# Third convolution: own-shift fetches of two chunks ahead of one burst of sixteen row transfers

## The chip, the cores and the metric

The kernel runs on one core of a Trainium2 chip. The metric is device time in microseconds (us) of one launch, the median of several runs. The core has TensorE (PE in the profile), VectorE (DVE), ScalarE (ACT), GpSimd (POOL) and SyncE (SP). SP and GpSimd issue the DMAs here: SP plain ones, GpSimd the indirect ones, whose rows are picked by an index in each partition.

## The reference, cut to what matters

A graph network with 6,250 nodes of 32 features and 200,000 edges sorted by destination: a spline-convolution layer (two small convolutions make a shift `t` per node, a third convolution uses it) and then a message-passing layer.

```
h = relu(layernorm(x))
h1 = elu(spline_conv(ones, row, col, basis, idx, stn1_w, stn1_b))
h2 = elu(spline_conv(h1, row, col, basis, idx, stn2_w, stn2_b))
t  = elu(h2 @ stn3_w + stn3_b) @ stn4_w + stn4_b
new_pseudo = clip(pseudo + t[col] - t[row], 0, 1)
basis2, idx2 = spline_basis(new_pseudo)
x = x + spline_conv(h, row, col, basis2, idx2, conv_w, conv_b)
...
mi = zeros.at[dst].add(e * x[src]);  mo = zeros.at[src].add(e * x[dst])
x = x + tanh-MLP(concat(mi, mo, h))
```

`t[row]` is an edge's own shift: all edges of one group of 16 slots have the same source node, so one fetched row per group gives it.

## The kernel before

The stages run one after the other, with barriers between them: `sort_edges`, `first_conv`, `second_conv`, `shift_network`, `third_conv`, `end_first_layer`, `bucket_rows` and `second_layer`. The change touches `third_conv` alone (lines 1765 to 2181).

`third_conv` works through 148 chunks (`NCK`) of 2,048 edge slots. Each engine has its own program, and semaphores are all that order them:

- **PE** (lines 2088 to 2181) does four rounds per chunk. In a round stand 32 matmuls of `outer_products` for chunk k+1 (line 2125), 16 of `weigh` for chunk k (line 2138) and 24 of `gather` for chunk k+3 (line 2105). Once per chunk it folds (2147), sums over nodes (2154) and spreads the own shifts of chunk k+3 (2113).
- **DVE** (1890 to 2035) is in chunk k with work for later chunks: `choose`, `own_shifts`, `take_own` and `move` for chunk k+3, `make_outer` and `make_basis` for chunk k+2, in two parts each. `own_shifts` (1957) reads the fetched own shifts, `take_own` (1962) copies what PE spread, and `make_basis` ends with `near_apart` (1982), which sets `s_basis`.
- **ACT** (2038 to 2085) copies PE's products out of PSUM (2042) and makes the hats.
- **SP** (1832 to 1860) waits in step k for the whole basis of chunk k-2 (`s_basis`, line 1848). Then it loads the near rows of chunk k (1849), waits until slot k mod 4 of the sending buffers is free, and loads eight rows per partition of edge data with their places (1852, 1853; `s_in`).
- **GpSimd** (1863 to 1887) does two unrelated things in one program, in a loop of four chunks (`DEEP`). It fetches the own shifts of chunk k from `t_rows` in HBM (1877) into one of two buffers, and it sends eight rows per partition of the edges into their buckets in HBM (`edges_b`, 1883), one indirect DMA for each row (`STEP` is 8). The sends serve the second layer and are not read in this stage. The fetch waits for `s_wide`, which tells that DVE has read the own shifts of chunk k-2, so that the buffer is free. The sends wait for `s_in`.

The order on GpSimd before, for each chunk: wait for the buffer, fetch; wait for the loads, eight sends. `second_conv` does some of the same sends (1453, sixteen in each pair of chunks of its last part) and, before them, gathers of 32 per pair of chunks (1431).

Of the kernel before, what the change touches and what calls it, by code (L numbers as in the profile page):

```python
# [58 lines left out]
STEP = 8  # L59
DEEP = 4  # L60
# [61 lines left out]
def held(pool, name, most):  # L122

    reg = pool.alloc_register(name)
    pool.reg_mov(reg, most)
    return pool.snap(reg)
# [1638 lines left out]
def third_conv(g, c, x, w_dram):  # L1765
# [19 lines left out]
    sending = Sending(g, c, "c3")  # L1785
# [4 lines left out]
    own_idx = sb("own_idx", [P, DEEP], U32)  # L1790
    own, own_wide, own_pos = sb("own_shift", [P, 2, 4]), sb("own_wide", [P, CH, 3]), sb("own_pos", [P, CH, 3])
# [7 lines left out]
    s_back, s_row, s_own = ([sm(f"{n}{h}") for h in range(2)] for n in ("near_in", "dst_rows", "own_shifts_sent"))  # L1799
    s_own_idx = sm("own_idx")  # L1800
    s_tick, s_pe_turn = sm("turns"), sm("pe_turns")
# [3 lines left out]
    s_wide, s_spread, s_taken = sm("own_wide"), sm("own_spread"), sm("own_taken")  # L1805
# [24 lines left out]
    with nc.Block() as block:  # L1830
        @block.sync
        def _(sp):
            sp.wait_ge(s_set, 1)
            sp.dma_start(weights[:, :, :], w_dram).then_inc(s_w, 16)
            sp.dma_start(g.x[:, 0:FULL_BLK, :], x[0:FULL_BLK * P, :].rearrange("(b p) f -> p b f", p=P)).then_inc(s_x, 16)
            sp.dma_start(g.x[0:REST, FULL_BLK, :], x[FULL_BLK * P:N, :]).then_inc(s_x, 16)

            def dst_rows(k, half):
                sp.dma_start(rows[:, half, :], g.dst_rows[ds(k * CH, CH), :].rearrange("t e -> (t e)").unsqueeze(0)
                             .to_broadcast([P, CH * P])).then_inc(s_row[half], 16)  # L1840

            def four_chunks(i, last):
                for n in range(DEEP):
                    k = i * DEEP + n
                    if not last or n < DEEP - 2:
                        sp.wait_ge(s_dst, k + 1)
                        dst_rows(k + 2, n % 2)
                    sp.wait_ge(s_basis, k * 2 + 2)
                    sp.dma_start(near[:, n % 2, :, :], near_rows[:, ds(k * CH, CH), :]).then_inc(s_back[n % 2], 16)
                    sp.wait_ge(sending.s_sent[n], i * (STEP * 16) + 16)  # L1850
                    step = i * DEEP + (EARLY + n)
                    sp.dma_start(sending.rows[:, n, :, :], edge_rows[:, ds(step * STEP, STEP), :]).then_inc(sending.s_in[n], 16)
                    sp.dma_start(sending.idx[:, n, :], edge_idx[:, ds(step * STEP, STEP)]).then_inc(sending.s_in[n], 16)

            for half in range(2):
                dst_rows(half, half)
            with sp.Fori(0, NCK // DEEP - 1) as i:
                four_chunks(i, False)
            four_chunks(NCK // DEEP - 1, True)
            sp.wait_ge(s_x, 32)  # L1860

        @block.gpsimd
        def _(pool):
            g.open_sent(pool, sending.s_sent)
            g.open_sent(pool, s_own, DEEP)
            last_node, last_place = held(pool, "last_node_of_t", NBLK * P - 1), held(pool, "last_place", P * NT - 1)
            with pool.Fori(0, NCK // DEEP) as i:
                for half in range(2):
                    pool.wait_ge(s_own[half], i * 32 + 16)
                pool.tensor_copy(own_idx[:, :], g.group_n[:, ds(i * DEEP, DEEP)]).then_inc(s_own_idx, 1)  # L1870
                pool.wait_ge(s_own_idx, i + 1)
                for n in range(DEEP):
                    k = i * DEEP + n
                    pool.wait_ge(s_own[n % 2], i * 32 + (n // 2 * 16 + 16))
                    pool.wait_ge(s_wide, k + 1)
                    pool.sem_inc(s_tick, 1)
                    pool.indirect_dma_start(own[:, n % 2, :], None, g.t_rows,
                                            bass.IndirectOffsetOnAxis(own_idx[:, n:n + 1], 0),
                                            bounds_check=last_node, oob_is_err=False).then_inc(s_own[n % 2], 16)
                    pool.wait_ge(sending.s_in[n], i * 32 + 32)  # L1880
                    pool.sem_inc(s_tick, 1)
                    for q in range(STEP):
                        pool.indirect_dma_start(g.edges_b, bass.IndirectOffsetOnAxis(sending.idx[:, n, q:q + 1], 0),  # L1883
                                                sending.rows[:, n, q, :], None, bounds_check=last_place,
                                                oob_is_err=False).then_inc(sending.s_sent[n], 16)
            for n in range(DEEP):
                pool.wait_ge(sending.s_sent[n], NCK // DEEP * (STEP * 16) + 16)

# [775 lines left out]
```

## Time and profile before

| | us |
|---|---|
| median of 3 runs | 11131.68 |
| lowest and highest run | 11116.91, 11136.16 |
| profiled execution, first to last instruction (span) | 14339.7 |
| PE busy in that span | 10087.9 (70%) |
| DVE, ACT busy | 7530.8 (53%), 4613.2 (32%) |
| GpSimd busy | 6070.4 (42%) |
| third convolution in the span | about 8530 to 11982 |

The profile gives no time of the profiled execution other than its span. The span is 3208 us longer than the median of the runs, so a duration of the profile isn't at once a duration of the runs. Start times are counted from the span's first instruction. "Issue" is idle time of an engine in which it waited for nothing that the profile shows.

### The profile page before, as it was taken

The numbers are of one execution on the slowest core, as the hardware profiler recorded it, in microseconds if no ns is written. First come the engines' busy times: TensorE is split into PE (matmuls) and PEld (weight loads), VectorE is DVE, ScalarE is ACT, GpSimd is POOL, SyncE is SP. The second block draws the span as 40 slices with busy tenths as digits, with TensorE's granted clock in tenths as the row PEclk, the third lists the DMA queues.
The fourth block names the chain that finished last, engine by engine and source line by source line (L and its number), as shares of the span: only waits on it lengthen the run. The fifth ranks groups of instructions, "written<-read, shape, count | busy, mean of one in ns | idle before, by whom it ended". The sixth has DMA issues, their size and how long they took to land. (4 is left out here: it accounts for less than half of the span.)

```text
span 14339.7 us, 414245 instructions
## 1 busy us (share of the span) xinstructions
PE 10087.9 (70%) x156361; PEld 8506.1 (59%) x156362; DVE 7530.8 (53%) x18528; ACT 4613.2 (32%) x11707; POOL 6070.4 (42%) x5974
## 2 busy tenths in 40 slices
PE   7566666657366666666677757777787776888888
PEld 7556555546244444444565545666666665888887
DVE  6667666757333333333344434444444444777776
ACT  0001000035122222222233322222222224777776
POOL 0477777743455545455433314444444441111111
PEclk6555555555566666666777767777777776555555
DMA  0222223310222222222211111111111112444443
GB/s 32 45 62 67 64 62 64 64 31 8 76 74 74 74 74 75 74 74 74 69 42 48 42 27 37 35 36 36 35 36 36 34 36 57 115 116 116 115 115 91
DMA packets 850556, 875.92 MB, mean 61 GB/s; under 512 B 629005, under 2 KB 632517, under 8 KB 849966
## 3 DMA queue, kind: packets, MB, share of 16 engines
q1 hardware_dynamic: 622830, 526.55, 13.2%
q0 software_dynamic: 227648, 348.32, 9.9%
q8 instruction: 50, 0.82, 0.0%
q14 instruction: 28, 0.23, 0.0%
HBM read 631.25 MB, written 135.27 MB: 53 GB/s over the span
## 5 line engine op out<-in xcount | busy, mean ns | idle before, releaser
L1611 PE MATMUL c_py<-c_products,c_weights 125*64 125x128 f32 x18944 | 1630.8, 302 | 675.0 <-issue 669.7
L769 POOL DMA_INDIRECT edges_by_rank<-rank_stage,rank_idx x1568 | 1844.7, 1176 | 602.0 <-issue 575.0
L1883 POOL DMA_INDIRECT edges_b<-c_send_rows,c_send_idx x1184 | 1277.9, 1079 | 1902.8 <-DMA c_send_idx<-edge_idx 1586.7
L1556 ACT ACTIVATE c_products<-c_pa 125x512 f32<-125x512 f32 x2368 | 1222.8, 602 | 2391.5 <-remote 1424.9
L1600 PE MATMUL c_pa<-c_near_apart,c_basis 32*125 32x128 f32 x18944 | 1247.0, 315 | 983.2 <-issue 734.5
L1611 PEld LDWEIGHTS c_py<-c_products,c_weights 125*64 125x64 f32 x18944 | 1236.6, 150 | 982.9 <-issue 927.2
L1431 POOL DMA_INDIRECT c_near_ranked<-h_rows,c_idx x1568 | 1597.9, 1019 | 478.1 <-issue 477.8
L1516 DVE TENSOR_TENSOR c_basis<-c_outer,c_hats 128x1000 f32<-128x1000 f32 x296 | 355.4, 1201 | 2745.9 <-PE c_pa L1600 2229.3
L1600 PEld LDWEIGHTS c_pa<-c_near_apart,c_basis 32*125 32x125 f32 x18944 | 958.5, 208 | 1297.4 <-issue 1295.7
L2042 ACT ACTIVATE c_products<-c_pa 125x256 f32<-125x256 f32 x2368 | 713.9, 386 | 2275.5 <-PE c_pa L2125 1411.0
L2125 PE MATMUL c_pa<-c_near_apart,c_basis 32*125 32x128 f32 x18944 | 1180.9, 334 | 242.7 <-issue 201.3
L289 PE MATMUL acc_s<-hot_col,hot_row 128*123 128x91 f16 x3136 | 768.4, 409 | 707.5 <-DVE same_a L668 416.0
L2488 PE MATMUL acc_mi_mo<-msg,hot_e 128*128 128x32 bf16 x8768 | 1152.6, 205 | 154.0 <-issue 153.0
L289 PEld LDWEIGHTS acc_s<-hot_col,hot_row 128*123 128x123 f16 x3136 | 723.4, 319 | 760.6 <-DVE same_a L668 442.3
L2125 PEld LDWEIGHTS c_pa<-c_near_apart,c_basis 32*125 32x125 f32 x18944 | 920.9, 223 | 422.1 <-issue 384.2
L748 PE MATMUL pg_s<-start_table,hot_turned 123*128 123x91 f32 x3136 | 1059.1, 450 | 136.3 <-issue 135.8
L2349 POOL DMA_DIRECT2D rows<-local_rows x548 | 298.9, 546 | 2000.3 <-DVE hot_d L2367 1819.7
L2488 PE MATMUL acc_mi_mo<-msg_low,hot_e 128*128 128x32 bf16 x8768 | 1143.2, 188 | 0.6 <-issue 0.6
L2488 PE MATMUL acc_mi_mo<-msg_rest,hot_e 128*128 128x32 bf16 x8768 | 1143.3, 188 | 0.0
L2105 PE MATMUL c_pt<-t_parts,c_dst_hot 128*128 128x78 bf16 x14208 | 850.3, 218 | 403.7 <-issue 351.1
L2105 PEld LDWEIGHTS c_pt<-t_parts,c_dst_hot 128*128 128x128 bf16 x14208 | 681.7, 110 | 637.6 <-issue 635.5
L2488 PEld LDWEIGHTS acc_mi_mo<-msg,hot_e 128*128 128x128 bf16 x8768 | 911.1, 104 | 212.2 <-issue 209.9
(402 smaller groups left out, 21318.8 us busy)
## 6 DMA issues: line engine op xcount, KB each, us to landing
rows<-local_rows POOLq DMA_DIRECT2D x548, 256.0 KB, 4.1
own_d<-hparts SPq DMA_DIRECT2D x2192, 48.0 KB, 2.9
hi_rows_in<-hi_rows SPq DMA_DIRECT2D x392, 256.0 KB
c_dst_rows_in<-dst_rows SPq DMA_DIRECT2D x148, 512.0 KB
near_by_rank<-c_near_ranked SPq DMA_DIRECT2D x98, 768.0 KB
rows_both<-hi_rows SPq DMA_DIRECT2D x196, 196.0 KB
near_h<-c_near_h SPq DMA_DIRECT2D x74, 512.0 KB
c_near<-near_h SPq DMA_DIRECT2D x148, 256.0 KB, 2.7
```

What stands on the lines that cost most here:

```text
L289: last = pe.matmul(acc[0:ROWS, bank, at:at + COLS], hot_row[:, half, :, q], hot_col[:, half, :, q], start=False, stop=True, skip_group_che ...
L748: pe.matmul(pg[:, half, bank, at:at + COLS], turned[0:ROWS, half, q * P:(q + 1) * P], table[0:ROWS, half, bank, at:at + COLS], start=True, ...
L769: pool.indirect_dma_start(g.ranked, bass.IndirectOffsetOnAxis(idx[:, r, q:q + 1], 0), stage[:, r, q, :], None, bounds_check=last_rank, oob ...
L1431: pool.indirect_dma_start(near[:, b, q, :], None, g.h1_rows, bass.IndirectOffsetOnAxis(idx[:, b, q:q + 1], 0), bounds_check=last_node, oob ...
L1556: last = act.activation(by_round[:, half, r, rnd], pa[0:K3, r, 0:TR * P].rearrange("p (f e) -> p f e", f=width), ACT.Copy)
L1600: last = pe.matmul(pa[0:K3, r, 0:TR * P].rearrange("p (f j s) -> p f j s", j=TR, s=2)[:, :, j, :], basis[at, q // HALF, q % HALF, :], apar ...
L1611: last = pe.matmul(py[n * width:(n + 1) * width, 0:P], weights[:, f, :], outer[:, half, f, :], start=(f < KP), stop=(f >= width - KP))
L1883: pool.indirect_dma_start(g.edges_b, bass.IndirectOffsetOnAxis(sending.idx[:, n, q:q + 1], 0), sending.rows[:, n, q, :], None, bounds_chec ...
L2042: last = act.activation(by_round[:, half, r, rnd], pa[0:K3, r, 0:TR * P].rearrange("p (e f i) -> p e f i", e=REP, f=F)[:, 0], ACT.Copy)
L2105: last = pe.matmul(pt[:, rnd % 2, j * 3 * HB:(j + 1) * 3 * HB], hot_lo[:, half, n // 3, t * P:(t + 1) * P], g.tparts[:, n % 3, n // 3, :], ...
L2125: last = pe.matmul(pa[0:K3, r, 0:TR * P].rearrange("p (e f j s) -> p e f j s", e=REP, j=TR, s=2)[:, :, :, j, :], basis[at, q // HALF, q % ...
L2488: last = pe.matmul(acc[:, ds(cols[(q - h * Q) * 2 + side] + (col + j * F), F)], hot_e[:, half, q, side, j * P:(j + 1) * P], part[:, half, ...
```

## The change

GpSimd's loop now goes by pairs of chunks. It fetches the own shifts of both chunks, then waits for the loads of both, and then issues the sixteen sends of both one after the other. Numbers of fetches, sends, loads and semaphore increments by DMAs stay, and so do all sizes and buffers; a turn counter (`s_tick`) is raised three times per pair instead of four. No other engine's program differs but for line numbers, which are two higher behind the change.

```
-                for n in range(DEEP):
-                    k = i * DEEP + n
-                    pool.wait_ge(s_own[n % 2], i * 32 + (n // 2 * 16 + 16))
-                    pool.wait_ge(s_wide, k + 1)
+                for pair in range(DEEP // 2):
+                    for n in (pair * 2, pair * 2 + 1):
+                        pool.wait_ge(s_own[n % 2], i * 32 + (n // 2 * 16 + 16))
+                        pool.wait_ge(s_wide, i * DEEP + (n + 1))
+                        pool.sem_inc(s_tick, 1)
+                        pool.indirect_dma_start(own[:, n % 2, :], None, g.t_rows,
+                                                bass.IndirectOffsetOnAxis(own_idx[:, n:n + 1], 0),
+                                                bounds_check=last_node, oob_is_err=False).then_inc(s_own[n % 2], 16)
+                    for n in (pair * 2, pair * 2 + 1):
+                        pool.wait_ge(sending.s_in[n], i * 32 + 32)
                     pool.sem_inc(s_tick, 1)
-                    pool.indirect_dma_start(own[:, n % 2, :], None, g.t_rows,
...
-                    pool.wait_ge(sending.s_in[n], i * 32 + 32)
-                    pool.sem_inc(s_tick, 1)
-                    for q in range(STEP):
-                        pool.indirect_dma_start(g.edges_b, bass.IndirectOffsetOnAxis(sending.idx[:, n, q:q + 1], 0),
...
+                    for n in (pair * 2, pair * 2 + 1):
+                        for q in range(STEP):
+                            pool.indirect_dma_start(g.edges_b, bass.IndirectOffsetOnAxis(sending.idx[:, n, q:q + 1], 0),
+                                                    sending.rows[:, n, q, :], None, bounds_check=last_place,
+                                                    oob_is_err=False).then_inc(sending.s_sent[n], 16)
```

In the built program, GpSimd's rows of the first two chunks of the loop (a row is an instruction, with its line and what it writes and reads; `x8` are eight of a kind; L1875 and L1880 or L1881 are the waits' register steps):

```order
 L1875 REGISTER_ALU
 L1877 DMA c_own_shift<-t_rows,c_own_idx 128x4
-L1880 REGISTER_ALU
-L1883 DMA edges_b<-c_send_rows,c_send_idx 280576x3 x8
 L1875 REGISTER_ALU
 L1877 DMA c_own_shift<-t_rows,c_own_idx 128x4
-L1883 DMA edges_b<-c_send_rows,c_send_idx 280576x3 x8
+L1881 REGISTER_ALU
+L1885 DMA edges_b<-c_send_rows,c_send_idx 280576x3 x16
```

The second fetch now stands ahead of the first chunk's sends, and all sixteen sends stand behind both fetches. The last two chunks of the loop, up to its branch back:

```order
 L1875 REGISTER_ALU
 L1877 DMA c_own_shift<-t_rows,c_own_idx 128x4
-L1883 DMA edges_b<-c_send_rows,c_send_idx 280576x3 x8
 L1875 REGISTER_ALU
 L1877 DMA c_own_shift<-t_rows,c_own_idx 128x4
-L1883 DMA edges_b<-c_send_rows,c_send_idx 280576x3 x8
+L1885 DMA edges_b<-c_send_rows,c_send_idx 280576x3 x16
 L1867 REGISTER_ALU
 L1867 COMPARE_AND_BRANCH
```

Here too the fetches come first. The fetches of the next pair, at the top of the loop, stand behind sixteen sends in a row, where before at most eight stood between two fetches.

## Rows read from the trace of the kernel before

**Rows 1.** Head of the page: the span.
```profile
span 14339.7 us, 414245 instructions
```
**Rows 2.** Waits, 8600 to 11975: waiter <- awaited, us in total, times, longest us.
```profile
POOL edges_b L1883 <- DMA c_send_idx<-edge_idx: 1565.3, 146, 25.3
```
**Rows 3.** Groups by line, GpSimd, 8600 to 11975: count | busy us, mean ns | idle before.
```profile
L1883 POOL DMA_INDIRECT edges_b<-c_send_rows,c_send_idx x1168 | 1261.8, 1080 | 1876.7 <-DMA c_send_idx<-edge_idx 1565.3 <-issue 311.5
L1877 POOL DMA_INDIRECT c_own_shift<-t_rows,c_own_idx x145 | 154.0, 1062 | 65.5 <-issue 62.8 <-POOL c_own_idx L1870 2.7
```
**Rows 4.** Line 2063, once per chunk, 8800 to 11800: ns, first and last start.
```profile
L2063 ACT ACTIVATE c_group_out<-c_small x131: 228/228/230, 8809.4 to 11796.2; 128x32 f32<-128x32 f32 x131
```
**Rows 5.** Timeline of PE, no sends under way: start us, us, engine, line.
```profile
10001.36 0.64 PE L2113 MATMUL c_small<-c_own_wide,c_of_group 128*128 128x48 f32 x2
...
10004.62 1.20 PE L2125 MATMUL c_pa<-c_near_apart,c_basis 32*125 32x128 f32 x32
10005.75 0.41 PE L2147 MATMUL c_small<-c_fold,c_group_out_turned 128*128 128x32 f32 x2
10006.09 0.64 PE L2138 MATMUL c_py<-c_products,c_weights 125*32 125x128 f32 x16
10006.66 1.01 PE L2105 MATMUL c_pt<-t_parts,c_dst_hot 128*128 128x78 bf16 x24
...
10008.69 0.63 PE L2154 MATMUL c_small<-c_group_out,c_node_hot 128*128 128x32 f32 x4
```
**Rows 6.** Timeline of PE during and just after eight sends.
```profile
10016.90 0.30 PE L2105 MATMUL c_pt<-t_parts,c_dst_hot 128*128 128x78 bf16 x4 [0.46 <-issue]
...
10022.08 2.16 PE L2125 MATMUL c_pa<-c_near_apart,c_basis 32*125 32x128 f32 x23 [0.15 <-issue]
10024.16 1.08 PE L2138 MATMUL c_py<-c_products,c_weights 125*32 125x128 f32 x16
```
**Rows 7.** Second convolution: line 1502, once per pair, and GpSimd's lines 1431, 1453.
```profile
L1502 DVE STREAM_TRANSPOSE c_near_h<-c_near_runs x43: 1917/1951/1983, 3923.7 to 6910.5; 128x1024 f32<-128x1024 f32 x43
L1502 DVE STREAM_TRANSPOSE c_near_h<-c_near_runs x22: 1922/1951/1973, 7279.1 to 8324.6; 128x1024 f32<-128x1024 f32 x22
...
8324.63 1.95 DVE L1502 STREAM_TRANSPOSE c_near_h<-c_near_runs 128x1024 f32<-128x1024 f32 x1
8353.93 1.96 DVE L1502 STREAM_TRANSPOSE c_near_h<-c_near_runs 128x1024 f32<-128x1024 f32 x1
...
L1431 POOL DMA_INDIRECT c_near_ranked<-h_rows,c_idx x1568 | 1597.9, 1019 | 478.1 <-issue 477.8
L1453 POOL DMA_INDIRECT edges_b<-c_send_rows,c_send_idx x384: 971/974/1983, 7136.8 to 8302.0; - x192
```
**Rows 8.** Timeline of DVE, SP and GpSimd around one chunk's basis, loads and sends.
```profile
10002.03 0.21 DVE L1962 COPY c_own_pos<-c_small 128x48 f32<-128x48 f32 x1
10004.36 0.69 DVE L1982 TENSOR_TENSOR c_near_apart<-c_near,c_real 128x512 f32<-128x512 f32 x1
10005.22 0.33 SPq L1849 DMA_DIRECT2D c_near<-near_h  x1
10006.27 0.33 SPq L1853 DMA_DIRECT2D c_send_idx<-edge_idx  x1
10009.22 1.01 POOL L1883 DMA_INDIRECT edges_b<-c_send_rows,c_send_idx  x1 [11.46 <-DMA c_send_idx<-edge_idx]
10011.91 1.88 POOL L1883 DMA_INDIRECT edges_b<-c_send_rows,c_send_idx  x1 [0.30 <-issue]
10014.72 0.20 DVE L1957 TENSOR_TENSOR c_own_wide<-c_own_shift,c_in_tile 128x48 f32<-128x48 f32 x1
10021.33 1.07 POOL L1877 DMA_INDIRECT c_own_shift<-t_rows,c_own_idx  x1 [0.90 <-issue]
```
**Rows 9.** Issue to landing: of c_near (8800 to 11800), and of a plain GpSimd load.
```profile
DMA to landing us min/median/max: 2.5/2.7/2.8
...
rows<-local_rows POOLq DMA_DIRECT2D x548, 256.0 KB, 4.1
```

More of the change, by code:

```diff
@@ L1871, in _ @@
                 pool.wait_ge(s_own_idx, i + 1)
-                for n in range(DEEP):
-                    k = i * DEEP + n
-                    pool.wait_ge(s_own[n % 2], i * 32 + (n // 2 * 16 + 16))
-                    pool.wait_ge(s_wide, k + 1)
-                    pool.sem_inc(s_tick, 1)
-                    pool.indirect_dma_start(own[:, n % 2, :], None, g.t_rows,
-                                            bass.IndirectOffsetOnAxis(own_idx[:, n:n + 1], 0),
-                                            bounds_check=last_node, oob_is_err=False).then_inc(s_own[n % 2], 16)
-                    pool.wait_ge(sending.s_in[n], i * 32 + 32)
-                    pool.sem_inc(s_tick, 1)
-                    for q in range(STEP):
-                        pool.indirect_dma_start(g.edges_b, bass.IndirectOffsetOnAxis(sending.idx[:, n, q:q + 1], 0),
-                                                sending.rows[:, n, q, :], None, bounds_check=last_place,
-                                                oob_is_err=False).then_inc(sending.s_sent[n], 16)
+                for pair in range(DEEP // 2):
[8 more added lines that the diff above has]
+                        pool.wait_ge(sending.s_in[n], i * 32 + 32)
+                    pool.sem_inc(s_tick, 1)
+                    for n in (pair * 2, pair * 2 + 1):
[3 more added lines that the diff above has]
+                                                    oob_is_err=False).then_inc(sending.s_sent[n], 16)
             for n in range(DEEP):
```

## The prediction

> **What bounds the kernel now.** I read the profile from the outside in. The span [rows 1] is 14339.7 us, and the median of the runs 11131.68 us: the profiled execution is 3208 us longer than the runs that count. Before any of its durations is used I ask where those 3208 us sit.
>
> The pace of the stage that changes comes from an instruction that runs once per chunk [rows 4]: (11796.2 - 8809.4)/130 = 22.98 us per chunk in the profile. What GpSimd does in it: 8 sends of 1.080 us with 311.5/1168 = 0.267 us before each, 1.347 us a send [rows 3], 10.8 us per chunk, and one fetch of 1.06 + 0.27 = 1.33 us. It waits 1565.3/146 = 10.7 us per chunk for the loads of the rows to send [rows 2]. By the profile GpSimd is half idle, and nobody reads in this stage what it sends.
>
> PE shows why a chunk takes 23 us. With no sends under way, a round is 1.20 + 0.64 + 1.01 us [rows 5], four rounds are 11.4 us, and with the spread (0.64), the fold (0.41) and the node sums (0.63) a chunk is 13.1 us. During sends PE gets only four matmuls done in about 0.76 us, most of it "issue" [rows 6]: it crawls and waits for nothing that the profile shows. The second convolution says the same in larger numbers [rows 7]: a pair of chunks takes (6910.5 - 3923.7)/42 = 71.1 us with 32 gathers, (8324.6 - 7279.1)/21 = 49.8 us with 16 sends, and 8353.93 - 8324.63 = 29.3 us with none. A send adds 20.5/16 = 1.28 us, a gather 41.8/32 = 1.31 us: as long as GpSimd issues, PE as good as stands.
>
> Do the timed runs have this crawl? Suppose they don't, and each stage goes at its next limit. The 49 gathering pairs of the second convolution would be bound by GpSimd: 34 transfers of 1.019 + 0.305 = 1.324 us, 45.0 instead of 71.1 us, 1279 us less. The 24 sending pairs would go from 49.8 to 29.3 us, 492 us less. The third convolution at PE's 13.1 us would save 148 x 9.88 = 1462 us. Together that is 3233 us, against 3208 us that have to be found. I take this as the likeliest: **the crawl belongs to the recording, and in the runs the chunk of the third convolution takes 13 to 15 us**, bound by PE. The lower end is PE's sum; the upper one leaves 300 us of the 3208 to the other stages, 300/148 = 2 us per chunk. I take 14.0 us.
>
> **The change part by part.** *Counts.* Sends, fetches, loads and their sizes stay. One counter step per pair falls away on GpSimd's sequencer; it lies in the 0.27 us before an instruction and I cost it at nothing; uncovered it would be under 0.3 us per pair.
>
> *The odd chunk's fetch moves ahead of the even chunk's sends*, 10.8 us earlier. Its buffer was freed a chunk before. No gain: in both orders DVE finds the odd chunk's shifts there.
>
> *The even chunk's sends move behind the odd chunk's loads.* They start up to one chunk later. SP needs their slot free only four steps later, some 56 us at 14 us a step, against about 14 + 11 + 3 us: hidden, and SP gets no new wait. If that cover went, SP's near loads would be queued behind the slot's wait.
>
> *What is queued behind them is the point.* The next pair's two fetches stand behind both waits and sixteen sends. With k the even chunk, the chain reads, in us:
> 1. The basis of chunk k-1 ends at 10004.36 + 0.69 = 10005.05; SP then issues the near load and the loads of rows and places, and the first send starts at 10009.22 [rows 8]: 4.17.
> 2. Sixteen sends at 1.347 [rows 3]: 21.55.
> 3. The fetch for chunk k+2: 1.06 [rows 3].
> 4. Its landing. No row has it. The nearest are a load by SP at 2.7 and a far larger load by GpSimd at 4.1 [rows 9]; below, 2.0. I take 2.7, since the fetch is small.
> 5. DVE widens the own shifts, 0.20 [rows 8], and PE spreads them, 0.64 [rows 5].
> 6. DVE copies the spread at 10002.03 and goes on to the end of the same chunk's second basis part at 10005.05 [rows 8]: 3.02.
>
> That is 33.3 us, and it ends at the basis of chunk k+1, two chunks after it began: it is closed. A pair can't be shorter, so **a chunk can't be shorter than 16.7 us**. Before, the same circle had eight sends: 22.6 us per pair, 11.3 per chunk, under PE's 13.1 and so without a price; GpSimd's own work, 12.1 us per chunk, was also below.
>
> In the profiled execution 16.7 is below 22.98, and I expect its span about where it was, 14,340 us. In the runs a chunk goes from 14.0 to 16.7 us. Over 70 of the 74 pairs (the loop fills and empties at its ends) that is 70 x 2 x 2.7 = 378 us: 11132 + 378 = **11510 us**, 3.4% slower.
>
> The ends of this case: sends at 1.28 us [rows 7], 2.0 us of landing and a chunk of 15.0 us before give 31.6/2 = 15.8, +112 us, 11244. Landing at 4.1 us, two sends in a burst at 1.88 us like the long one [rows 8], and 13.1 us before give 36.3/2 = 18.2, +709 us, 11841; all of that at once is unlikely, and I end this case at 11720.
>
> For the fetch's landing alone the Trainium skill has a price ("DMA: Bandwidth & Descriptors", section on the anatomy of a DMA from GpSimd): about 2.0 us of fixed cost per transfer. By it the circle would be 32.6 us a pair and the time 11457 us; no row here shows it.
>
> **The rivals.** *No change (11132 us).* The runs have a chunk longer than 16.7 us, or GpSimd issues faster in them. If the crawl is real, a chunk stays near 23 us and the circle of 33.3 us per pair hides in 46 us. If the 0.27 us before each send is recording too, the circle is 33.3 - 16 x 0.27 = 29.0 us, 14.5 per chunk, about what I give PE. For it speaks that every row of the profile shows the crawl and none shows its absence in a run. Against it: the 3208 us have to come from somewhere, and a faster GpSimd would save 49 x 34 x 0.3 = 500 us more in the second convolution than the runs have left. The point from which it decides is the chunk in the runs: above 16.7 us nothing happens.
> A rule stands on this side. The Trainium skill ("Runtime: NRT & Kernel Launch", section on the preamble and postamble) says that a profile's total time is some 6.2 us above the execution time, whatever the kernel; by it the runs would have the profile's chunk of 23 us, and the change would cost nothing. The 3208 us of this case speak against it.
>
> *Faster (about 11050 us).* If the crawl holds in the runs, one burst of sixteen instead of two of eight removes one run-out per pair. After the last send PE stays slow for a while: 23 matmuls in 2.16 us where 32 take 1.20, then 16 in 1.08 where they take 0.64 [rows 5, 6]: 1.3 + 0.4 = 1.7 us, at most 74 x 1.7 = 126 us. I put it at 80 us, since no row shows how long the run-out of a burst of sixteen is. It needs the crawl in the runs, as the case before.
>
> *The burst does not form*: GpSimd could still stop between the chunks. It can't, since both waits stand ahead of the first send.
>
> **How the numbers follow.** A measurement of this kernel can tell about 0.2%, 22 us, from no change. The circle decides in the runs: 0.72, all of it slower by more than 0.2%. No change: 0.14. Faster by the run-outs: 0.14. The likeliest gives 11510 us, its own range 11240 to 11720. To leave out no more than 2 in 10, the range goes down to 11110 and takes in no change and small gains.
>
> **What would show it right or wrong.** In the profile of the changed kernel GpSimd should show sixteen sends in a row and half as many waits for loads, 74, with two fetches close together ahead of them. If its chunk is still near 23 us while the timed runs are slower by some hundred microseconds, the circle in the runs is the reason that is left; DVE's wait for the own shifts should appear in it only where the chunk is short. If the runs are unchanged, their chunk is above 16.7 us, and my reading of the 3208 us is wrong. If the profile's span itself grows by hundreds of microseconds, the price lies in something that I have not seen, such as the loads of SP meeting the longer burst.

## The result and the profile after

| | before | after |
|---|---|---|
| median of 4 runs on the same chip, us | 11126.03 | 11722.40 |
| lowest and highest run | 11116.91, 11136.16 | 11717.83, 11730.29 |
| ratio | | 1.0536 [1.0521, 1.0551] |

The change costs 596 us, 5.4%. The profiled execution of the changed kernel took 11719.97 us, its span is as long as the runs, so its rows are durations of the runs, which [rows 1] were not:

```profile
span 11718.2 us, 414171 instructions
```

The instruction that ACT runs once per chunk, in the whole stage (answers to [rows 4], two lines further down in the code): its duration, then its first and last start.

```profile
L2065 ACT ACTIVATE c_group_out<-c_small x148: 197/232/233, 6862.6 to 9357.1; 128x32 f32<-128x32 f32 x148
```

The same in the stage's steady part, 6950 to 9300:

```profile
L2065 ACT ACTIVATE c_group_out<-c_small x137: 231/232/233, 6956.5 to 9288.0; 128x32 f32<-128x32 f32 x137
```

That is (9288.0 - 6956.5)/136 = **17.14 us per chunk**, 34.3 per pair. What the stage waits for, and GpSimd's groups, both from 6900 to 9300 (answer to [rows 2, 3]):

```profile
POOL edges_b L1885 <- issue: 965.4, 1121, 9.9
...
PE c_small L2115 <- DVE c_own_wide L1959: 542.2, 140, 9.1
DVE c_own_wide L1959 <- DMA c_own_shift<-t_rows,c_own_idx: 419.9, 70, 8.1
```

```profile
L1885 POOL DMA_INDIRECT edges_b<-c_send_rows,c_send_idx x1121 | 1220.4, 1089 | 965.4 <-issue 965.4
L1877 POOL DMA_INDIRECT c_own_shift<-t_rows,c_own_idx x140 | 144.8, 1034 | 63.5 <-issue 32.1 <-POOL c_own_idx L1870 31.4
```

DVE now waits for the fetched own shifts, in every second chunk (70 of 140), 419.9/70 = 6.0 us each time. PE waits for the spread behind them, 542.2/140 = 3.9 us per chunk on average. GpSimd's own waiting for loads is put down to "issue" here: of 965.4 us some 1121 x 0.30 = 336 are the usual gap before a send, and the other 629 us are 9.0 us per pair. Seen from GpSimd alone there seems to be room; seen from the circle there is none. One turn of it in the timeline (start us, us, engine and line; in brackets the idle time before):

```profile
8010.18 0.68 DVE L1984 TENSOR_TENSOR c_near_apart<-c_near,c_real 128x512 f32<-128x512 f32 x1
8011.04 0.33 SPq L1849 DMA_DIRECT2D c_near<-near_h  x1
8012.10 0.33 SPq L1853 DMA_DIRECT2D c_send_idx<-edge_idx  x1
8014.88 1.01 POOL L1885 DMA_INDIRECT edges_b<-c_send_rows,c_send_idx  x1 [8.96 <-issue]
...
8035.86 0.98 POOL L1885 DMA_INDIRECT edges_b<-c_send_rows,c_send_idx  x1 [0.31 <-issue]
8036.83 0.22 POOL L1870 COPY c_own_idx<-group_n 128x4 uint32 x1
8037.94 1.06 POOL L1877 DMA_INDIRECT c_own_shift<-t_rows,c_own_idx  x1 [0.90 <-POOL c_own_idx L1870]
...
8040.46 0.21 DVE L1959 TENSOR_TENSOR c_own_wide<-c_own_shift,c_in_tile 128x48 f32<-128x48 f32 x1 [6.08 <-DMA c_own_shift<-t_rows,c_own_idx]
...
8040.73 0.66 PE L2115 MATMUL c_small<-c_own_wide,c_of_group 128*128 128x48 f32 x2 [7.09 <-DVE c_own_wide L1959]
...
8041.32 2.08 PE L2127 MATMUL c_pa<-c_near_apart,c_basis 32*125 32x128 f32 x32
...
8044.59 0.68 DVE L1984 TENSOR_TENSOR c_near_apart<-c_near,c_real 128x512 f32<-128x512 f32 x1
```

From the end of one basis (8010.86) to the end of the basis two chunks on (8045.27) it is 34.41 us, and the next turn begins there. This turn has GpSimd's copy of the indices in it, which comes once in two pairs; from first send to first send it takes 34.55 us, the next turn, without the copy, 33.66 us.

### The profile page after: what moved, and what is told of

It reads as the page before. It is cut to its first block and busy times, and to the rows that moved or that the text cites. A ratio compares the mean times of both kernels' runs of the same rounds, so it can differ in the third digit from the quotient of the medians.

```text
span 11718.2 us, 414171 instructions
## 1 busy us (share of the span) xinstructions
PE 8365.9 (71%) x156361; PEld 7570.6 (65%) x156362; DVE 7576.2 (65%) x18528; ACT 4595.2 (39%) x11707; POOL 6143.8 (52%) x5974
## 5 line engine op out<-in xcount | busy, mean ns | idle before, releaser
L1431 POOL DMA_INDIRECT c_near_ranked<-h_rows,c_idx x1568 | 1673.8, 1067 | 477.7 <-issue 477.7
L1600 PE MATMUL c_pa<-c_near_apart,c_basis 32*125 32x128 f32 x18944 | 745.4, 294 | 1014.4 <-DVE c_near_apart L1519 912.2
L1600 PEld LDWEIGHTS c_pa<-c_near_apart,c_basis 32*125 32x125 f32 x18944 | 638.5, 195 | 1134.1 <-issue 1134.1
L1611 PE MATMUL c_py<-c_products,c_weights 125*64 125x128 f32 x18944 | 1219.1, 284 | 0.0
L1611 PEld LDWEIGHTS c_py<-c_products,c_weights 125*64 125x64 f32 x18944 | 1074.6, 142 | 58.0 <-issue 0.2
L2490 PEld LDWEIGHTS acc_mi_mo<-msg_rest,hot_e 128*128 128x128 bf16 x8768 | 1016.6, 116 | 0.0
L1501 DVE STREAM_TRANSPOSE c_near<-c_near_runs 128x2048 f32<-128x2048 f32 x74 | 271.5, 3669 | 1068.3 <-DMA c_near_runs<-near_by_rank,c_near_run_idx 1031.2
L2375 DVE TENSOR_SCALAR hot_e<-iota,edges 128x256 bf16<-128x256 f16 x4384 | 926.1, 280 | 0.0
L2490 PEld LDWEIGHTS acc_mi_mo<-msg_low,hot_e 128*128 128x128 bf16 x8768 | 916.4, 105 | 0.7 <-issue 0.7
L730 ACT ACTIVATE rank_stage<-row_of_edge 128x32 f32 (+1 forms) x196 | 44.9, 229 | 1999.8 <-DMA edges_by_rank<-rank_stage,rank_idx 1996.0
```

What stands on the lines that cost most here:

```text
L1431: pool.indirect_dma_start(near[:, b, q, :], None, g.h1_rows, bass.IndirectOffsetOnAxis(idx[:, b, q:q + 1], 0), bounds_check=last_node, oob ...
L1600: last = pe.matmul(pa[0:K3, r, 0:TR * P].rearrange("p (f j s) -> p f j s", j=TR, s=2)[:, :, j, :], basis[at, q // HALF, q % HALF, :], apar ...
L1611: last = pe.matmul(py[n * width:(n + 1) * width, 0:P], weights[:, f, :], outer[:, half, f, :], start=(f < KP), stop=(f >= width - KP))
L2375: dve.tensor_scalar(hot_e[:, half, q, side, :], g.iota16[:, :], g.edges[:, ds(i * (2 * SH) + (half * SH + q), 1), column:column + 1] .rear ...
L2490: last = pe.matmul(acc[:, ds(cols[(q - h * Q) * 2 + side] + (col + j * F), F)], hot_e[:, half, q, side, j * P:(j + 1) * P], part[:, half, ...
```

## The experiments

My theory: the sixteen sends stand between two fetches in GpSimd's queue, and so close the circle; before, eight did, and PE hid it. Rivals: the burst itself is dear (DMAs, PE's crawl); the joint wait costs without the queue; GpSimd's work was the bound before.

**1. The kernel before, recorded once more.** No edit.

> The kernel before, unchanged, recorded again. If PE's crawl during GpSimd's issues belonged to that one recording, the span falls from 14339.7 to the time of the runs, about 11125 us, a pair with 32 gathers in the second convolution from 71.1 to some 46 us, and a chunk of the third convolution from 22.98 to about 13.1 us (the changed kernel's third stage took 2587 us in its profile, the runs differ by 596 us, so 1991 us are left for 148 chunks and the ends). If the crawl comes with every recording of this order of the program, the span is again about 14340 us.

The execution took 11142.62 us:

```profile
span 11140.8 us, 414245 instructions
```

The chunk in the whole stage, and in 6900 to 8600; the pair of the second convolution with gathers and with sends [rows 7]:

```profile
L2063 ACT ACTIVATE c_group_out<-c_small x148: 197/232/233, 6870.5 to 8778.1; 128x32 f32<-128x32 f32 x148
```

```profile
L2063 ACT ACTIVATE c_group_out<-c_small x130: 232/232/233, 6912.7 to 8599.1; 128x32 f32<-128x32 f32 x130
```

```profile
L1502 DVE STREAM_TRANSPOSE c_near_h<-c_near_runs x38: 1854/1864/1880, 3943.8 to 5690.8; 128x1024 f32<-128x1024 f32 x38
L1502 DVE STREAM_TRANSPOSE c_near_h<-c_near_runs x27: 1864/1957/1975, 5833.0 to 6577.0; 128x1024 f32<-128x1024 f32 x27
```

The chunk takes (8599.1 - 6912.7)/129 = 13.07 us, the pairs 47.2 and 28.6 us. The crawl belonged to that one recording, not to the kernel. GpSimd in 6900 to 8600, by group and then its longest gap before a send:

```profile
L1883 POOL DMA_INDIRECT edges_b<-c_send_rows,c_send_idx x1041 | 1158.8, 1113 | 317.5 <-issue 316.0 <-DVE c_own_wide L1957 1.5
L1877 POOL DMA_INDIRECT c_own_shift<-t_rows,c_own_idx x130 | 159.4, 1226 | 58.6 <-issue 29.9 <-DMA c_send_idx<-edge_idx 28.7
```

```profile
POOL edges_b L1883 <- issue: 316.0, 1036, 0.3
```

With 7.1 us of copies these rows fill 1158.8 + 317.5 + 159.4 + 58.6 + 7.1 = 1701 of 1700 us. Busy time and gaps fill any window; what counts is that no gap before a send is longer than 0.3 us. GpSimd waits for no loads here. PE in the same window: its waits, and start and end us, length, busy time (count) of PE, PEld, DVE, ACT and POOL, granted clock, DMA share, GB/s:

```profile
PE c_small L2113 <- DVE c_own_wide L1957: 100.6, 130, 0.9
PE c_pa L2125 <- ACT c_products L2042: 60.5, 130, 0.5
```

```profile
6900.00:8600.00 1700.00, 1538.98 (x38500) 1307.22 (x38501) 1477.80 (x2992) 846.45 (x3120) 1324.20 (x1203) 1.00 0.24 63
```

PE is busy 1538.98/1700 of 13.07 = 11.83 us per chunk, and waits 100.6/130 = 0.77 us for the own shifts and 60.5/130 = 0.47 us for ACT. Whether GpSimd sets the pace, or PE's path with these waits, experiments 8 to 11 ask.

**2. Both fetches first, but each chunk's own wait ahead of its own eight sends.**

```diff
+                    fetch(pair * 2)
+                    fetch(pair * 2 + 1)
                     for n in (pair * 2, pair * 2 + 1):
+                        loaded(n)
+                        send(n, 0, STEP)
```

> One part of the change alone: both fetches ahead, but each chunk's loads are waited for by themselves and its eight sends follow at once. Theory (the circle through the basis of chunk k-1, the sends behind it, the next fetch and the own shifts): only eight sends stand in the circle, 34.3 - 10.8 = 23.5 us per pair, under PE's 26.2, so the time is that of before, 11126 us within 30. Rival (the early fetch of the odd chunk itself costs, by waiting for its buffer in front of the even chunk's sends): slower than before, up to 11700 us.

11152.11 us against 11141.40, 1.0009 [0.9999, 1.0018]; 13.11 us per chunk. Fetching both first costs nothing that can be told.

**3. The joint wait, but the odd fetch between two times eight sends.**

```diff
+                    fetch(pair * 2)
                     for n in (pair * 2, pair * 2 + 1):
+                        loaded(n)
+                    send(pair * 2, 0, STEP)
+                    fetch(pair * 2 + 1)
+                    send(pair * 2 + 1, 0, STEP)
```

> The other part alone: the loads of both chunks are waited for together, but the odd chunk's fetch stays between the two groups of eight sends, so no sixteen sends stand in a row. Theory (circle): all sixteen sends and now a fetch more stand in the circle, about 35 to 36 us per pair, 11730 to 11850 us. Rival (sixteen small transfers in a row crowd the DMA queues): the row is broken, so the time falls back towards before, 11130 to 11400 us.

11895.61 us, 1.0675 [1.0657, 1.0693], somewhat above the expected time; 18.07 us per chunk. Waits, 6950 to 8650:

```profile
POOL edges_b L1882 <- DMA c_send_idx<-edge_idx: 536.1, 52, 12.5
...
DVE c_own_wide L1968 <- DMA c_own_shift<-t_rows,c_own_idx: 391.4, 52, 8.3
```

So the early odd fetch of the change isn't what costs: without it the pair is 36.1 us, 1.8 longer than in the change. Of these a fetch and its gap, 1.06 + 0.31 = 1.37 us, stand between the two times eight sends and so within the circle; the other 0.4 us are open.

**4. The burst of sixteen kept, the next pair's two fetches issued ahead of the wait for loads** (indices filled two columns ahead, a prologue of two fetches, the last pass written out).

```diff
+                        if n < width:
+                            fetch(i * DEEP + (n + 2), n, i * 32 + (pair * 16 + 32))
                     for n in (pair * 2, pair * 2 + 1):
                         pool.wait_ge(sending.s_in[n], i * 32 + 32)
...
+            for k in range(2):
+                fetch(k, k + 2, 16)
```

> The changed kernel with its bursts of sixteen kept, but the fetches of the next pair issued ahead of the wait for the loads instead of behind the sends. Theory (circle): the sends no longer stand between a basis and the next fetch; the chunk goes back to PE's limit, 11126 us within 40. Rival (the burst of sixteen itself, by the DMA queues or by GpSimd's and DVE's meeting): stays at 11720 us.

11141.35 us, 0.9998 [0.9989, 1.0008]; 6950 to 8650:

```profile
L2081 ACT ACTIVATE c_group_out<-c_small x130: 228/229/230, 6958.8 to 8645.3; 128x32 f32<-128x32 f32 x130
```

The same sends in the same bursts behind the same joint wait, and a chunk is back at 13.07 us. The burst costs nothing; what stands behind it in the queue does. Rival one is gone, and rival two as well.

**5 and 6. Two, or four, of the even chunk's sends ahead of the joint wait.**

```diff
+                    loaded(pair * 2)
+                    send(pair * 2, 0, 2)
+                    loaded(pair * 2 + 1)
+                    send(pair * 2, 2, STEP)
+                    send(pair * 2 + 1, 0, STEP)
```

(With 4 in place of 2 in the sixth.)

> The changed kernel, but the first two of the even chunk's sends start after its own loads, and only fourteen stand behind the wait for the odd chunk's loads. Theory (circle): two sends of 1.09 + 0.30 us leave the circle, 34.3 - 2.8 = 31.5 us per pair, 73 x 2.8 = 204 us less than the changed kernel: 11738 (1.0536 of the 11141 us that the kernel before has today) - 204 = 11534 us. Rival (a fixed cost of a joint wait, or of a burst beyond some length): stays within 50 us of 11738, or falls all the way.

> The same with four sends ahead and twelve behind the wait. Theory (circle): 34.3 - 5.6 = 28.7 us per pair, 73 x 5.6 = 409 us less than the changed kernel: 11330 us. Rival: as for two, no straight line through 0, 2, 4 and 8 sends.

11532.24 us, 1.0367 [1.0350, 1.0385], and 11321.65 us, 1.0178 [1.0161, 1.0195], against 11125.29; 31.75 and 28.75 us per pair. With 0, 2, 4 and 8 sends ahead of the wait the ratio is 1.0536, 1.0367, 1.0178 and 1.0009. Two sends are worth 188 to 210 us as long as the circle rules. The expected times stood on 11141 us for the kernel before; on this day's 11125 they are 11518 and 11313, some 15 and 9 us under the measured ones. DVE's wait for the own shifts falls with the sends, from 6.0 us each time in the changed kernel to 3.6 and 1.7 us; 6950 to 8650, fifth and sixth:

```profile
DVE c_own_wide L1969 <- DMA c_own_shift<-t_rows,c_own_idx: 194.2, 54, 5.3
```

```profile
DVE c_own_wide L1969 <- DMA c_own_shift<-t_rows,c_own_idx: 100.3, 60, 3.5
```

**7. The change, with SP loading rows and places ahead of its wait for the basis.**

```diff
-                    sp.wait_ge(s_basis, k * 2 + 2)
-                    sp.dma_start(near[:, n % 2, :, :], near_rows[:, ds(k * CH, CH), :]).then_inc(s_back[n % 2], 16)
                     sp.wait_ge(sending.s_sent[n], i * (STEP * 16) + 16)
...
+                    sp.wait_ge(s_basis, k * 2 + 2)
+                    sp.dma_start(near[:, n % 2, :, :], near_rows[:, ds(k * CH, CH), :]).then_inc(s_back[n % 2], 16)
```

> The changed kernel with its joint wait and burst of sixteen; on SP the loads of rows and places are issued ahead of the wait for the basis, the near load stays behind it. Theory (the circle is closed by SP's wait for the basis in front of those loads): the start of a burst no longer hangs on the own shifts of the pair before; 11141 us within 40. Rival (the joint wait or the burst costs by itself): stays near 11738 us.

11234.10 us, 1.0095 [1.0078, 1.0112], 13.77 us per chunk. A miss: 109 us above before. The circle's other side is confirmed, since cutting its link from the basis to the loads gives back 487 of the 596 us; the rest is not explained by it. Waits, 6950 to 8650:

```profile
POOL edges_b L1885 <- issue: 374.0, 987, 4.2
...
DVE c_own_wide L1959 <- DMA c_own_shift<-t_rows,c_own_idx: 63.3, 56, 3.2
```

GpSimd still stops for loads, up to 4.2 us, and DVE for shifts. SP has an earlier wait in the step, for the destinations that DVE makes (line 1929). One stop in the timeline:

```profile
8044.70 0.58 DVE L1929 TENSOR_TENSOR c_dst_hot_hi<-c_dst_num_hi,dst_hi 128x416 f16<-128x416 f16 x1
...
8045.47 0.33 SPq L1839 DMA_DIRECT2D c_dst_rows_in<-dst_rows  x1
8046.01 0.33 SPq L1850 DMA_DIRECT2D c_send_rows<-edge_rows  x1
8046.52 0.33 SPq L1851 DMA_DIRECT2D c_send_idx<-edge_idx  x1
...
8050.24 1.01 POOL L1885 DMA_INDIRECT edges_b<-c_send_rows,c_send_idx  x1 [2.45 <-issue]
```

SP goes on 0.19 us after DVE's line 1929 has ended (8045.28), and the loads for which GpSimd stops follow at once. So they still hang on DVE, now by the destinations. I suppose that a longer circle goes through this wait and costs the 109 us; no run tried that.

**8. The kernel before with seven of eight sends.**

```diff
-                    for q in range(STEP):
+                    for q in range(SENDS):
```

> The order of before, with seven of the eight sends of each chunk; the eighth row of each step is left out, so an eighth of the edges of this stage never reach their buckets. It asks what bounds the chunk of before, 13.07 us in the second recording, where GpSimd sends at 1.113 + 0.305 us and waits for no loads at all. If GpSimd bounds it: up to 1.42 us per chunk less, 10930 us, or as far as PE's own limit lets it. If PE bounds it (13.1 us by my sum of its rounds): 11141 us within 25.

11128.66 us, 1.0003 [0.9994, 1.0013]; 13.11 us per chunk. GpSimd now stops for loads (170.9 us in 82 waits, 6950 to 8650), and the chunk is no shorter: though full in experiment 1, GpSimd isn't what alone sets the pace of before. Rival three, as the only bound, is gone.

**9. The kernel before, DVE's `own_shifts` ahead of the node mask.**

```diff
+                if left >= 3:
+                    own_shifts(k + 3, 1 - half, i + 2 + half)
                 dve.tensor_scalar(hot[:, :], g.iotaf[:, 0:2 * P], g.node_in[:, ds(k, 1)], None,
                                   ALU.is_equal).then_inc(s_hot, 1)
-                if left >= 3:
-                    own_shifts(k + 3, 1 - half, i + 2 + half)
```

> The order of before on GpSimd; on DVE own_shifts is moved one instruction earlier, ahead of the node mask of line 2007 (0.35 us). In the second recording of before PE waits 0.69 to 0.86 us per chunk for own_shifts, and 0.47 us for ACT. If PE's path alone bounds the chunk: about 0.35 us less per chunk, 148 x 0.35 = 52 us, 11080 us. If GpSimd, which is busy or between two issues all the time, bounds it as well: 11130 us within 15.

11129.53 us against 11134.94, 0.9992 [0.9983, 1.0001]; 13.04 us per chunk. That is the time expected if GpSimd bounds the chunk as well as PE, and experiment 11 bears it out. DVE now waits for fetched shifts, which it did not before (6950 to 8650):

```profile
DVE c_own_wide L1957 <- DMA c_own_shift<-t_rows,c_own_idx: 21.9, 33, 1.0
```

**10. The ninth, with GpSimd's copy of indices made two columns at a time behind a fetch,** so that its own semaphore wait is hidden.

```diff
+                    if n % 2 == 0 and not (last and n == 2):
+                        pool.wait_ge(s_own[1], i * 32 + (n // 2 * 16 + 16))
+                        pool.tensor_copy(own_idx[:, 2 - n:4 - n], g.group_n[:, ds(i * DEEP + (n + 2), 2)]).then_inc(s_own_idx, 1)
```

> The same, and on GpSimd the four indices of a loop are copied two by two behind a fetch, not at the head of the loop, where 0.22 us of copy and 0.90 us of waiting for it stand ahead of the next fetch; about 0.7 us per four chunks less on GpSimd, 26 us in all. If GpSimd is the second bound: 11100 us, and below the time of the move on DVE alone. If only PE bounds: the same as the move on DVE alone.

11106.24 us, 0.9975 [0.9966, 0.9984]; 6950 to 8650:

```profile
L2072 ACT ACTIVATE c_group_out<-c_small x132: 232/232/233, 6952.8 to 8638.3; 128x32 f32<-128x32 f32 x132
```

12.87 us per chunk, and 28.7 us less than the kernel before; 23 us of them against the ninth, where 26 were expected.

**11. The ninth with seven of eight sends** (both edits above).

> The move on DVE together with seven sends of eight (the eighth row of each step is left out, so an eighth of this stage's edges never reach their buckets). GpSimd then has 1.4 us of room per chunk. It shows PE's own gain by the move: 11080 us if PE waits 0.35 us less per chunk, 11125 us if another wait on PE takes its place.

11091.69 us, 0.9954 [0.9940, 0.9967]; 12.76 us per chunk. One send less is worth nothing in the kernel before and 38 us behind the ninth's edit: before, PE's path with its waits (13.11 us in experiment 8) and GpSimd's queue (13.07) stood at the same limit, and only both edits together move the chunk.

## Why the prediction's mechanism was right and its size was not

**The mechanism was right.** A fetch queued behind a wait for loads and sixteen sends, two chunks long: experiments 4 to 6 show that the place of the fetches and the number of sends between them set the price, and by experiments 2 and 4 (1.0009 and 0.9998) the rest of the change has none that can be told.

**The reading of the recording was right.** I had found 3233 us of crawl to take out, of 3208 that had to go; experiment 1 shows the kernel without it. "As long as GpSimd issues, PE as good as stands" was too strong: in the burst that began at 10009.22 [rows 8] PE still did 22 matmuls in 0.97 us at 10012.82. And then I expected the changed kernel's profile to keep a span of about 14,340 us with a chunk near 23 us. That was wrong: its span is 11718.2 us. I took a trouble of one recording for one of every recording.

**The step that failed is the size of the sum: 378 us forecast, 596 measured, and 11722.40 us is 2 us above the range.** In the stage the first and last chunk lie 2494.5 us apart after and 1907.6 before: 587 us, 147 x (16.97 - 12.98). (As wholes the two recordings lie 577 us apart, so the split is good to some 20 us.) Against 70 x 2 x 2.7 three terms fail, the first one most.

- *"I take 14.0 us"* for the chunk before: measured 13.07. PE's rows had added up to 13.1 [rows 5]. I raised it because 300 us of the 3208 might be left to other stages; nothing in the rows asked for that, and the 3233 us had used 13.1. 0.93 x 140 = 130 us. That the 13.1 fits is partly luck: the rows of [rows 5] overlap by some 0.07 us each, the spread took 0.64 us there and 0.42 in experiment 1, and PE's waits are missing. PE's own work is 11.83 us, and 1.24 us of waits make up the chunk.
- *The circle, 33.3 us a pair, 16.7 a chunk:* measured 34.3 and 17.14. 0.44 x 140 = 62 us.
- *70 of the 74 pairs:* the price of a steady chunk, 17.14 - 13.07 = 4.07 us, goes 144 times into the 587 us, not 140 times. That is the rest of the stage, 587 - 378 - 130 - 62 = 17 us.

**The circle link by link**, forecast and measured in the turn above:

| link | forecast | measured |
|---|---|---|
| basis ends to first send | 4.17 | 4.02 |
| sixteen sends | 21.55 | 21.95 |
| copy of indices and its wait (every second pair) | 0 | 1.11 |
| fetch starts to DVE widens | 3.76 | 2.52 |
| DVE widens to basis ends | 3.86 | 4.81 |

Three of the errors have names. I had not asked what the copy (0.22 us) and the wait for it (0.90) cost in the circle. The fetch instruction was counted twice: 2.7 us [rows 9] run from the issue of a load, and I added them behind the 1.06 us of the fetch instruction. From the end of that instruction to DVE it is 8040.46 - 8039.00 = 1.46 us; from its start it is 2.52, and over all fetches of the changed kernel (line 1877) the median from issue to landing is 2.5 us, near the 2.7 of SP's load:

```profile
DMA to landing us min/median/max: 2.4/2.5/7.0
```

The Trainium skill's 2.0 us ("DMA: Bandwidth & Descriptors", anatomy of a DMA from GpSimd), which I had added behind the instruction as well, lies between the two ways to count. And the last link is longer by 0.95 us, mostly because PE comes out of its wait at the lower clock. The windows of that turn: start and end us, length, busy time (count) of PE, PEld, DVE, ACT and POOL, granted clock, DMA share, GB/s.

```profile
8034.00:8035.00 1.00, 0.00 (x0) 0.00 (x0) 0.39 (x1) 0.00 (x0) 0.70 (x2) 1.00 0.03 2
...
8036.00:8037.00 1.00, 0.00 (x0) 0.00 (x0) 0.00 (x0) 0.00 (x0) 1.00 (x2) 0.79 0.03 2
8037.00:8038.00 1.00, 0.00 (x0) 0.00 (x0) 0.00 (x0) 0.00 (x0) 0.10 (x2) 0.50 0.03 2
...
8044.00:8045.00 1.00, 1.00 (x19) 0.65 (x12) 1.00 (x2) 0.86 (x4) 0.00 (x0) 0.50 0.00 0
...
8047.00:8048.00 1.00, 1.00 (x30) 0.84 (x30) 1.00 (x1) 0.38 (x2) 0.00 (x0) 1.00 0.60 179
```

PE stands for 7 us; in that time the granted clock falls from 1.00 (2.4 GHz) to 0.50 (1.2 GHz). The round that releases the basis then takes 2.08 us where the round at 8049.33, back at the upper level, takes 1.15:

```profile
8049.33 1.15 PE L2127 MATMUL c_pa<-c_near_apart,c_basis 32*125 32x128 f32 x32
```

The same round in the link that I had read [rows 8] took 1.25 us (from 10001.93), so that 0.83 of the 0.95 us are this round. In the stage the clock averages 0.86 after and 1.00 in experiment 1: the wait that the circle makes lengthens the circle. The price had stood in my rows. The slow rounds after the sends [rows 6], 16 matmuls in 1.08 us and not 0.64, ran at the lower level too:

```profile
10021.00:10026.00 5.00, 4.51 (x54) 3.56 (x54) 2.33 (x4) 1.38 (x5) 1.07 (x1) 0.50 0.02 0
```

I had used them for the run-out of the rival "faster" alone, and not for PE's wait in the circle.

**GpSimd's own work** I had put at 12.1 us per chunk, below PE. It is 13.07 (sends of 1.113 us with 0.305 before each, fetches of 1.226 with 0.45), as long as PE's path. This moved nothing in the price of the change, but it was the reason that taking the own shifts earlier alone gained nothing (experiment 9).

**The rivals.** No change and faster both needed the crawl in the runs; it isn't there. Nor does GpSimd issue faster than in [rows 3]: in experiment 1 it takes 0.305 us before each send. The burst did form.

## What to carry to other kernels

A wait for work that nobody reads soon is free only if nothing that is needed stands behind it in the same queue: follow the circle from the wait through the queue and back, and count everything between two fetches. Where rows of an undisturbed stretch give a pace, take it and not a middle value, but leave out what overlaps in them and put in the waits. Before any duration is used, hold the span against the runs, and if they differ, hold no later recording to the same fault.

## What the runs showed of the hardware

Two recordings of the same kernel had spans of 14339.7 and 11140.8 us, while timed executions lay within 0.2% of their median. In the long one PE got, during sends, only four matmuls done in some 0.76 us [rows 6]; in the other GpSimd sent all the time and PE was busy for 90% of the steady part. What made the difference is open.

GpSimd's sends differ in length from recording to recording: 1.080 us each in the crawling one [rows 3], 1.113 us in the second, 1.089 us in the changed kernel, and, at the ends, 1.059 us in experiment 3 and 1.174 us in experiment 11. They don't simply follow the pace of the stage: experiment 7 has 1.138 us with 13.77 us per chunk, the tenth 1.101 us with 12.87. What sets them is open.
